# A gated feed-forward kernel: both direct groups of 512 tokens placed ahead of the three Strassen groups, and the projection weight prepared in halves

## The reference

```python
q_emb = relu(cond @ W3 + b3)                                  # [16, 512]
v = (256 * x + x.sum(axis=1, keepdims=True)) * q_emb[:, None, :]
h = relu(v @ W2 + b2)                                         # [16, 256, 512]
h_q = where(h > 0.33, 0.5, where(h < -0.33, -0.5, 0.0))
w = where(weight > 0.2, 0.6, where(weight < -0.2, -0.6, 0.0)) + rram
out = x + einsum('bsd,od->bso', h_q, w)
```

## Time and profile before

| what | value |
|---|---|
| median of 3 runs | 198.66 us (198.41 to 199.66) |
| the profiled execution, its own time | 198.73 us |
| its span, first to last instruction | 196.9 us |
| TensorE busy in matrix products | 179.1 us (91%) |
| VectorE, ScalarE, GpSimd busy | 114.9, 60.8, 23.2 us |
| mean granted TensorE clock | 0.957 of full speed |

### The profile page before, as it was taken

One profiled execution on the slowest core, in us unless ns is written; L12 is line 12 of the kernel. 1 busy time (PEld: TensorE's weight loads), 2 busy tenths in 40 slices (PEclk: granted clock), 3 DMA queues, 4 the chain that ended last, 5 costly groups with the idle time before them and its releaser, 6 DMA issues.

```text
span 196.9 us, 2207 instructions
## 1 busy us (share of the span) xinstructions
PE 179.1 (91%) x804; PEld 133.9 (68%) x804; DVE 114.9 (58%) x133; ACT 60.8 (31%) x157; POOL 23.2 (12%) x26
## 2 busy tenths in 40 slices
PE   7989999496992099999999999999999999999994
PEld 2759995144450099886766878767668788988994
DVE  1847999687799614459975544499325322322333
ACT  2044445500099990202998202019400000000000
POOL 2004900004951900000000000000000000000000
PEclk9957999789999579999999999999999999999999
DMA  5999999999000999766112114911121137113124
GB/s 164 295 223 222 212 218 223 230 263 186 7 3 7 322 267 221 251 221 258 53 57 106 53 53 143 336 57 53 53 107 53 57 99 275 53 55 109 54 107 160
DMA packets 31002, 28.99 MB, mean 147 GB/s; under 512 B 1536, under 2 KB 22288, under 8 KB 30992
## 3 DMA queue, kind: packets, MB, share of 16 engines
q1 hardware_dynamic: 30320, 28.58, 55.1%
q10 hardware_dynamic: 608, 0.28, 0.6%
q0 software_dynamic: 64, 0.00, 0.0%
HBM read 20.47 MB, written 8.39 MB: 147 GB/s over the span
## 4 chain that ended last, share of the span: by engine, by line
PE 68%; DVE 14%; SPq 5%; DMA 4%; issue 3%; POOL 2%; ACT 2%; POOLq 1%; DVEq 0%
PE out_ps L674 31%; PE hid_ps L757 7%; DVE xT L363 6%; PE hid_ps L612 5%; PE hid_ps L648 4%; PE hid_ps L660 4%; PE hid_ps L627 4%; DMA x_in<-in_x 4%; PE hid_ps L605 4%; PE hid_ps L640 3%; PE hid_ps L667 3%; DVE x_sum L394 2%; SPq L195 2%; POOL wT_lo L287 2%; DVE wT L526 1%
## 5 line engine op out<-in xcount | busy, mean ns | idle before, releaser
L674 PE MATMUL out_ps<-wT_lo,hid 128*128 128x256 f32 x252 | 70.6, 319 | 8.3 <-POOL wT_lo L287 8.3
L674 PE MATMUL out_ps<-wT_hi,hid 128*128 128x256 f32 x252 | 62.3, 286 | 0.0
L674 PEld LDWEIGHTS out_ps<-wT_lo,hid 128*128 128x128 f32 x252 | 49.1, 195 | 12.4 <-POOL wT_lo L287 9.1
L674 PEld LDWEIGHTS out_ps<-wT_hi,hid 128*128 128x128 f32 x252 | 49.2, 195 | 4.8 <-issue 4.8
L481 DVE SCALAR_TENSOR_TENSOR x_res<-out_ps,x_res 128x512 f32<-128x512 f32 x31 | 21.3, 687 | 29.5 <-PE out_ps L674 29.5
L306 ACT ACTIVATE xT<-xT,coef,q_scale 128x256 f32<-128x256 f32 x64 | 33.2, 590 | 13.2 <-DVE coef L396 12.8
L363 DVE STREAM_TRANSPOSE xT<-x_in 128x1024 f32<-128x1024 f32 x15 | 30.6, 2047 | 3.8 <-DMA x_in<-in_x 3.8
L317 ACT ACTIVATE junk<-xT,q_emb 128x256 bf16<-128x256 f32 x40 | 19.8, 495 | 38.8 <-DVE xT L363 38.8
L612 PE MATMUL hid_ps<-xT,w_sb 128*128 128x512 f32 x24 | 13.0, 684 | 2.6 <-ACT e L327 2.6
L757 PE MATMUL hid_ps<-xT,w_sb 128*128 128x512 f32 x32 | 14.8, 606 | 0.0
L648 PE MATMUL hid_ps<-t_sum,s_mix 128*128 128x512 f32 x24 | 11.4, 595 | 1.6 <-DVE n L447 1.6
(11 more groups left out here) (64 smaller groups left out, 160.6 us busy)
## 6 DMA issues: line engine op xcount, KB each, us to landing
out<-x_res SPq DMA_DIRECT2D x31, 256.0 KB, 2.0
x_in<-in_x SPq DMA_DIRECT2D x28, 256.0 KB, 7.3
x_res<-in_x SPq DMA_DIRECT2D x3, 2048.0 KB, 8.4
x_res<-in_x SPq DMA_DIRECT2D x2, 1024.0 KB, 7.8
w_sb<-in_L_cond_W SPq DMA_DIRECT2D x4, 256.0 KB, 6.1
x_res<-in_L_ffn_weight SPq DMA_DIRECT2D x4, 256.0 KB, 7.0
x_res<-in_L_ffn_rram_variation SPq DMA_DIRECT2D x4, 256.0 KB, 7.0
w_sb<-in_L_cond_W SPq DMA_DIRECT2D x1, 512.0 KB, 4.2
```

Source lines behind the costliest of these rows:

```text
L674: mm = nc.tensor.matmul(bank[:, cols], hid[:, g % 2, k, c * P:(c + 1) * P], w[:, k, cols], start=(k == 0 and w is wT_lo), stop=(k == KD - ...
```

## The change

The groups become: direct over batches 0 and 1, direct over batches 2 and 3, Strassen 1 to 3 over batches 4 to 15. All groups of `hid` and `x_res` now hold eight tiles, and `slot_of` puts batch n in slot n // 4 % 2. The first eight projections are split over the products of Strassen group 1. VectorE sums batches 0, 1, 2, 3, 5 and 7, ScalarE the others, 4 and 6 among them. The two compares of the weight move ahead of batch 7; its transposes, copies and low parts go by halves of 256 columns, each with its own count in the semaphores, and the first projection waits for one half at a time. `token_sums_34` becomes `token_sum_3` and `token_sum_4` with `sum_16` between them. The sums of W2 blocks on GpSimd wait for four coefs instead of two. Pair 3 of x is loaded ahead of weight and rram, and `load_res(0)` (now eight tiles) ahead of pair 4. TensorE gets a filler product after each of the four q products and five instead of two behind them.

```diff
-    WARM, WARM_2 = 10, 2
+    WARM, WARM_2 = 10, 5
+    VECTOR_SUMS = (0, 1, 2, 3, 5, 7)
 # SyncE
             load_pair(2)
+            sp.wait_ge(s_tr, 1)
+            load_pair(3)
...
-            sp.wait_ge(s_tr, 1)
-            load_pair(3)
+            load_res(0)
             sp.wait_ge(s_tr, 3)
             load_pair(4)
-            load_res(0)
 # GpSimd
-            pool.wait_ge(s_coef, 2)
+            pool.wait_ge(s_coef, 4)
...
-            for k in range(KD):
-                pool.wait_ge(s_whi, k + 1)
-                nc.gpsimd.tensor_tensor(wT_lo[:, k], ...)
+            for h, cols in enumerate(COLS):
+                pool.wait_ge(s_whi, h + 1)
+                nc.gpsimd.tensor_tensor(wT_lo[:, :, cols], wT[:, :, cols], wT_hi[:, :, cols].bitcast(F32),
+                                        ALU.subtract).then_inc(s_wlo, 1)
 # ScalarE
-            for n in range(5):
+            for n in range(4):
                 scale_summed(n)
+            sum_and_scale(4)
+            scale_summed(5)
+            sum_and_scale(6)
             copy_p1(1, 0)
-            scale_summed(5)
+            scale_summed(7)
             copy_p1(1, 1)
-            sum_and_scale(6)
-            sum_and_scale(7)
+            for h, cols in enumerate(COLS):
+                act.wait_ge(s_wT, h + 1)
+                nc.scalar.copy(wT_hi[:, :, cols], wT[:, :, cols]).then_inc(s_whi, 1)
+            for n in range(8, 12):
+                sum_and_scale(n)
 # VectorE, new
+            def transpose_weight(h):
+                rows = slice(h * OB // 2, (h + 1) * OB // 2)
+                dve.wait_ge(s_wsum, 2 * h + 2)
+                nc.vector.transpose(wT[:, :, COLS[h]]..., w_in[:, rows]...).then_inc(s_wT, 1)
+            prepare(2); prepare(3)
+            quantize(0, 0); quantize(0, 1); quantize(0, 2); quantize(0, 3)
+            transpose_batch(4); prepare(5); quantize(1, 0); transpose_batch(6)
+            dve.wait_ge(s_w, QUADS * DMA)
+...
+            quantize(1, 1); prepare(7); quantize(1, 2); quantize(1, 3)
+            token_sums_12(1); c11(1, 0); c11(1, 1); token_sum_3(1); sum_16(1, 0); token_sum_4(1)
+            transpose_weight(0); sum_167(1, 0); c22(1, 0); transpose_weight(1)
+            c21(1, 0); sum_16(1, 1); c12(1, 0); transpose_batch(8); sum_167(1, 1); c22(1, 1)
+            finish(0, 0); transpose_batch(9); finish(0, 1); finish(0, 2); c21(1, 1)
+            transpose_batch(10); finish(0, 3); finish(0, 4); transpose_batch(11); finish(0, 5)
+            c12(1, 1); finish(0, 6); finish(0, 7)
 # TensorE
+                if m == KD - 1:
+                    mm.then_inc(s_q_ps, 1)
+                nc.tensor.matmul(out_ps[3][:], warm[:, 0:P], warm[:], start=True, stop=True)
...
+            for m in range(KD):
+                pe.wait_ge(s_xs, 4 * KD)
+                pe.wait_ge(s_cls_hid, m + 1)
+                for k in range(KD):
+                    mm = nc.tensor.matmul(hid_ps[m][:], chunk_columns(w2_sb[:, k], m), xT[:, 0, k, TOK:], ...)
+                mm.then_inc(s_cls, 1)
...
             p7(1, 1)
+            project(0, 0)
+            project(0, 1)
+            project(0, 2)
             p4(1, 1)
+            project(0, 3)
+            project(0, 4)
+            project(0, 5)
             p3(1, 1)
-            pe.wait_ge(s_wlo, KD)
-            for c in range(4):
-                project(FIRST, c)
+            project(0, 6)
+            project(0, 7)
...
-            for m in range(KD):
-                pe.wait_ge(s_xs, KD * B)
...
-                    mm = nc.tensor.matmul(hid_ps[m][:], chunk_columns(w2_sb[:, k], m), xT[:, LAST % 2, k, 0:TOK],
...
-                project(3, 2 * m)
-                project(3, 2 * m + 1)
-            for c in range(3):
+            for c in range(TILES - 1):
                 project(LAST, c)
```

More of the change, by code:

```diff
@@ L67, in adaln_ffn_kernel @@
     rram_split = rram.rearrange("(n t) (q f) -> q t n f", t=BLK, q=QUADS)
[L70 to L73, removed]
+    GROUPS = B // 4
+    LAST = GROUPS - 1
+    TILES = 8
+    VECTOR_SUMS = (0, 1, 2, 3, 5, 7)
+    SCALAR_SUMS = tuple(n for n in range(B) if n not in VECTOR_SUMS)
     ctx = ExitStack()
@@ L327, in copy_p1 @@
                 nc.scalar.activation(e1[:, j], hid_ps[j][:], ACT.Copy, scale=-1.0).then_inc(s_e1, 1)
-            for n in range(5):
+            for n in range(4):
                 scale_summed(n)
+            sum_and_scale(4)
+            scale_summed(5)
+            sum_and_scale(6)
             copy_p1(1, 0)
-            scale_summed(5)
+            scale_summed(7)
             copy_p1(1, 1)
-            sum_and_scale(6)
-            sum_and_scale(7)
[L336 to L345, removed]
+            for h, cols in enumerate(COLS):
[3 more added lines that the diff above has]
+                sum_and_scale(n)
+            copy_p1(2, 0)
+            copy_p1(2, 1)
+            for n in range(12, 16):
+                sum_and_scale(n)
+            copy_p1(3, 0)
+            copy_p1(3, 1)
         @block.vector
@@ L391, in prepare @@
                 s, cols = slot_of(n)
+                done = VECTOR_SUMS.index(n)
                 transpose_batch(n)
@@ L425, in token_sums_34, with token_sum_4 @@
                                         ALU.subtract).then_inc(s_tsum, 1)
+            def token_sum_4(g):
+                s = g % 2
                 if g > 1:
@@ L496, in _ @@
             prepare(3)
-            quantize(FIRST, 0)
-            prepare(4)
-            quantize(FIRST, 1)
-            quantize(FIRST, 2)
-            prepare(5)
-            quantize(FIRST, 3)
+            quantize(0, 0)
+            quantize(0, 1)
+            quantize(0, 2)
+            quantize(0, 3)
+            transpose_batch(4)
+            prepare(5)
+            quantize(1, 0)
+            transpose_batch(6)
+            dve.wait_ge(s_w, QUADS * DMA)
+            nc.vector.tensor_scalar(w_gt, w_in, TH_W, SC_W, ALU.is_gt, ALU.mult).then_inc(s_wq, 1)
+            dve.wait_ge(s_wq, 1)
+            nc.vector.tensor_scalar(w_in, w_in, -TH_W, SC_W, ALU.is_lt, ALU.mult).then_inc(s_wq, 1)
+            quantize(1, 1)
+            prepare(7)
+            quantize(1, 2)
+            quantize(1, 3)
             dve.wait_ge(s_th, 1)
@@ L507, in _ @@
             c11(1, 1)
-            token_sums_34(1)
-            dve.wait_ge(s_w, QUADS * DMA)
-            nc.vector.tensor_scalar(w_gt, w_in, TH_W, SC_W, ALU.is_gt, ALU.mult).then_inc(s_wq, 1)
+            token_sum_3(1)
             sum_16(1, 0)
-            dve.wait_ge(s_wq, 1)
-            nc.vector.tensor_scalar(w_in, w_in, -TH_W, SC_W, ALU.is_lt, ALU.mult).then_inc(s_wq, 1)
+            token_sum_4(1)
+            transpose_weight(0)
             sum_167(1, 0)
             c22(1, 0)
+            transpose_weight(1)
             c21(1, 0)
             sum_16(1, 1)
-            transpose_batch(6)
             c12(1, 0)
-            transpose_batch(7)
+            transpose_batch(8)
             sum_167(1, 1)
             c22(1, 1)
-            for h in range(2):
-                rows = slice(h * OB // 2, (h + 1) * OB // 2)
-                dve.wait_ge(s_wsum, 4)
-                nc.vector.transpose(wT[:, :, h * D // 2:(h + 1) * D // 2].rearrange("p j (n t) -> p n j t", t=BLK),
-                                    w_in[:, rows].rearrange("p n (r j) -> p n j r", r=BLK)).then_inc(s_wT, 1)
-                if h == 0:
-                    c21(1, 1)
+            finish(0, 0)
+            transpose_batch(9)
+            finish(0, 1)
+            finish(0, 2)
+            c21(1, 1)
+            transpose_batch(10)
+            finish(0, 3)
+            finish(0, 4)
+            transpose_batch(11)
+            finish(0, 5)
             c12(1, 1)
-            transpose_batch(8)
-            transpose_batch(9)
-            for c in range(4):
-                finish(FIRST, c)
+            finish(0, 6)
+            finish(0, 7)
             for g in (2, 3):
@@ L622, in p6 @@
                 elif g == 1:
[L623 removed]
+                    pe.wait_ge(s_cls_hid, KD + 3)
                 else:
```

155 lines of the change are left out of this document (64 added, 91 removed).

## The result

The changed kernel takes 182.51 us (median of 4 runs, 181.96 to 183.02) where the kernel before takes 198.55: a ratio of 0.918, 95% interval 0.9135 to 0.9226. Measured again on another chip it was 182.81 us and 0.9184 (0.9138 to 0.9231). The profiled execution took 182.18 us with a span of 180.4. Forecast: 183.1, from 180.5 to 187.0.

The account below looks back on a forecast made before the run. TensorE was taken as the bound, with all that can be won in the first 69 us. Its end at 28.7 + 148.6 + 1.4 = 178.7, + 2.6 + 1.83, gave 183.1 us; range 180.5 to 187.0.

Parts of the forecast that it names:

- The work left when nothing waits: TensorE from the second direct group's start to its end: 14.2 + 3 x 39.68 + 15.3 = 148.6 us.
- S: Time at which the second direct group starts on TensorE: taken as 28.7 us, between 27.7 and 29.9.
- the gap: TensorE's wait before P6 as GpSimd's weight operations slow VectorE's token sums: 0 to 2.5 us, taken as 1.4.
- the middle case: Clock up when the first direct product starts: it takes 7.5 instead of 9.9 us, second direct group at 28.4.
- The 0.55 us won at coef 2: On VectorE, coef 2 no longer stands 0.55 us behind GpSimd, so batch 3 is scaled 0.5 us earlier.
- The band 181.3 to 184.6: Forecast time with the wait before P6 and the second direct group's start at their bounds; chance 0.55.
- The tightest point: P6 on TensorE wants the first two token sums at 50.5 us, ready at 50.4: slack 0.1 us.
- The weight chain: Halves of wT_lo ready at 60.3 and 63.8 us; 14.2 us of direct product cover the 8.3 us wait, 1.4 spare.
- The slower rival: VectorE's queue waits for the loaded weight: each us after 38.2 costs one, gain gone at 54; chance 0.02.
- C: VectorE's slacks of 0.4 to 1.4 us fail, wT_lo late again: 4.1 + 1.6 us, 188.8; chance 0.09.
- D: Idle time only moves: TensorE stops among the first eight projections, 10 us or more, 197 to 200; chance 0.02.
- A: Wait before P6 at its upper bound and the clock falls in it: + 1.1 and + 1.8 us, 186.0; chance 0.20.

Follow-up runs that it names:

- e8: Changed kernel with the sums of batches 4 and 6 back on VectorE; 185.98 us, ratio 0.9332 to the kernel before.
- e9: Changed kernel with pair 3 of x loaded behind weight and rram, as before; 186.15 us, ratio 0.9353 to the kernel before.
- e7: Changed kernel with load_res(0), 2 MB, ahead of weight and rram in SyncE's order; 185.04 us, ratio 0.9242 to the kernel before.
- e3: Changed kernel with GpSimd's four weight additions waiting until the first two token sums are done; 181.64 us, ratio 0.9132 to the kernel before.
- e10: Changed kernel with the weight compares ahead of batch 6's transpose and GpSimd's additions behind the first two token sums; 181.87 us, ratio 0.9149 to the kernel before.
- e5: Changed kernel with the weight loaded ahead of pair 3 and its two compares ahead of batch 4's transpose; 183.02 us, ratio 0.9167 to the kernel before.
- e2: Changed kernel with the weight compares back behind token_sum_3 and the weight transposes behind c22(1, 1); 193.69 us, ratio 0.9734 to the kernel before.
- e6: Changed kernel with the first eight projections behind all of Strassen group 1; 182.97 us, ratio 0.9162 to the kernel before.
- e1: Changed kernel with the fillers as before, none in the q group and two behind it; 183.68 us, ratio 0.9235 to the kernel before.

## Why the prediction was right

**The work left when nothing waits.** 28.06 + 148.6 + 1.07 = 177.7, measured 177.74. The last 95 us could be taken over from the trace of before as they were, and that is the mechanism. The agreement to a tenth in the rest is luck: the direct group took 13.75 instead of 14.2 us, and the first Strassen group 1.07 + 0.45 more than 39.68, most of the 0.45 at P2. The 3.55 us per column block came from a direct group in which each product stood behind projections. P4, which reads W2 as that group does, takes 1.83 us behind a projection and 1.72 without (69.88 and 55.54 in the chain above), and the direct group at its new place has no projections in it. The forecast of 183.1 is 0.9 us over the 182.18 of the profiled execution, 0.6 from S and 0.3 from the gap.

**S.** Forecast 28.7 between 27.7 and 29.9; measured 28.06 in the profile, 27.7 to 29.0 in the other profiles with all fillers. By windows of half a us the clock fell before 10.0 us and was back between 13.0 and 13.5, near the middle case; in the other profiles that have a fall on record it was back between 12.4 (e8) and 15.5 us (e9), and S went with it. The 0.55 us won at coef 2 came as forecast (0.16 us now). It did not set S in this profile, where nothing waited at the start of the second group, but in the repeated one TensorE waited 0.40 us there for the scaling of batch 3 (S = 28.40). The band 181.3 to 184.6 was said to have the gap and S at their bounds; both at their bounds together give 180.7 to 185.4.

**The tightest point.** P6 behind `token_sums_12`, with a slack of 0.1 us, was named, and it is where the changed kernel waits. But there were two such points: the second copy of P1, to which the prediction gave 0.2 us (48.5 for 48.7), has no slack either, and when VectorE is late it is the one that TensorE waits for (e7, e8, e9). The wait before P6 was forecast as 1.4 us for the overlap with GpSimd and was 1.07 and 1.92 in the two profiles; e3 and e10 take the overlap away and the wait with it, so this cause is shown. The Trainium skill's sentence on the shared interfaces (GPSIMD Engine Reference, 1. Specifications) names both kinds of VectorE instruction, those with two SBUF inputs and those in a 2-port mode; I had used only the first. e5's compares, 1.39 and 1.76 instead of 1.17 and 1.23 us with one input each, may be the second kind; that they were in such a mode no row here shows.

**What I had mis-sized, all small.** Coef 7 behind GpSimd costs more than nothing: it makes ScalarE's scaling and the second copy of P1 late, P2 took 2.11 instead of 1.72 us. And I priced only VectorE's side of the overlap; GpSimd's additions take 1.9 us longer (1.0 in the repeated profile). The halves of `wT_lo` were there at 59.8 and 63.2, forecast 60.3 and 63.8 at a later S.

**The weight chain and the move.** The 8.3 us are gone for the reason given, and e2 shows it: with compares and transposes at their old place 11 of the 16 us are lost again. What I did not see is that the split of the first projections, which I laid out step by step, is worth nothing that can be measured (e6).

**The slower rival.** Its slope, one us for one us of late weight, is what e7's profile shows (2.0 for a wait of 1.94), but from the time at which VectorE is ready for the compare, 36.8 to 37.6 us, and not from 38.2; its break-even at a landing of 54 us was not tried. Rivals C and D did not occur; of A the repeated profile shows the longer wait, 1.92 us, without the fall of the clock. A took the fall from one gap of 2.64 us. The length alone does not decide it: the clock stayed at 1.00 through and behind the 2.85 us in e9, and fell behind the 3.12 us in e8.

## What to carry to other kernels

When one engine is the bound for most of the span, write the new time as its work left after one point plus the waits before it, with the rows of the old trace; then lay out each helper's queue by hand and look for the smallest slack. Independent work in front of a stage pays in full only if the long preparation chain is started as early as that work: with the chain left at its old place in the helper's queue, 11 of 16 us were lost here. Place GpSimd's operations beside VectorE's transposes (2.07 us beside them, 2.06 without), reductions (1.22) and reads of PSUM (0.70 each for two in a row, either way), not beside its sums of two SBUF tensors (2.17 instead of 1.22).

## What the hardware showed that was not expected

The granted clock in the record was not always that of the array in the first 10 us. In the changed kernel's profile and in e3's the record says 1.00 from 7.0 to 7.5 us, but fillers that start then take 0.38 us in one and 0.59 in the other:

```profile
7.31 0.38 PE L591 MATMUL out_ps<-warm 128*128 128x512 bf16 x1
```
```profile
7.09 0.59 PE L592 MATMUL out_ps<-warm 128*128 128x512 bf16 x1
```
```profile
7.00:7.50 0.50, 0.50 (x4) 1.00 0.92 328
12.00:12.50 0.50, 0.50 (x2) 1.00 1.24 225
```

Both windows lines are e3's (the stretch, its length, TensorE's busy time and instructions, the granted clock, the DMA share, GB/s): its record has no fall at all, and its mean is 1.00. From one filler to the next are 1.13 us in e3 (8.22 after 7.09) and 0.96 in the other (8.27 after 7.31). In the changed kernel's profile a filler takes 0.59 us where the record says 0.50 (at 10.19 us), so the 0.59 in e3 is what a filler takes at 1.2 GHz. e1 says the same more plainly: a record of 1.00 from 4 to 20 us and a mean of 0.998, while its first direct product takes 10.08 us, longer than the 9.90 that the kernel before took with 0.50 on record. So a mean clock near 1 need not mean that the clock was up in the first us of a kernel, and the durations of equal instructions are the better witness. The mean does not forecast the time either: the two executions of the changed kernel with 1.000 took 182.84 and 183.02 us, those with 0.991 took 181.96 and 182.18, but in the repeated run 1.000 went with 182.44 to 182.84 and 0.981 to 0.991 with 182.05 to 183.41.
